# Attention on one core: the values' product of two quads of heads in one run, and eight buffers of probabilities in place of four

## The reference, cut to what matters

```python
def _L1_attn_ref(hidden_states, Wq, bq, Wk, bk, Wv, bv, Wo, bo):
    HEADS, HEAD_DIM = 16, 8
    ...                                   # q, k, v = linear(hidden_states), split into heads
    scores = jnp.einsum('bqhd,bkhd->bhqk', q * SCALE, k)
    probs = jax.nn.softmax(scores.astype(jnp.float32), axis=-1).astype(scores.dtype)
    out = jnp.einsum('bhqk,bkhd->bqhd', probs, v).reshape(b, s, d)
    return out @ Wo.T + bo
```

## Time and profile before

| | |
|---|---|
| median of 3 runs | 1103.3 us (1101.86 to 1104.05) |
| span of the profiled execution, first to last instruction | 1072.1 us |
| outside of the span, by the median | 31.2 us |
| PE busy | 963.4 us, 90% of the span |
| DVE, ACT, POOL busy | 706.6, 640.7, 707.7 us |
| `values` (L1518), matmul records | 2048, 141.6 us busy |

### The profile page before, as it was taken

How to read it: one execution, slowest core, us unless ns; L and a number is a source line. 1 busy time by engine, 2 the same in 40 slices (tenths; PEclk the granted TensorE clock), 3 DMA queues, 4 the chain that set the end, 5 groups by cost and what they waited for, 6 DMA issues and landing times. The chain is left out here.

```text
span 1072.1 us, 29674 instructions
## 1 busy us (share of the span) xinstructions
PE 963.4 (90%) x9857; PEld 717.1 (67%) x9858; DVE 706.6 (66%) x1509; ACT 640.7 (60%) x1320; POOL 707.7 (66%) x1531
## 2 busy tenths in 40 slices
PE   6999999689989999459999999999999999963776
PEld 5888888479956666335767777777777777632554
DVE  5778787685534444236788887788787788735752
ACT  4666766422224434126788888888888888762552
POOL 4677676467735555567688888888888888534003
PEclk9999999799999999757999999999999999996999
DMA  8600000131123332134444544445454445302000
GB/s 315 262 3 2 2 2 2 45 104 53 50 74 83 81 83 70 52 106 132 122 137 140 149 130 141 127 137 150 124 149 124 124 134 140 99 17 61 12 3 21
DMA packets 88837, 100.91 MB, mean 94 GB/s; under 512 B 10654, under 2 KB 74366, under 8 KB 88318
## 3 DMA queue, kind: packets, MB, share of 16 engines
q1 hardware_dynamic: 83454, 87.97, 27.9%
q0 software_dynamic: 5248, 11.15, 3.2%
HBM read 61.78 MB, written 36.47 MB: 92 GB/s over the span
## 5 line engine op out<-in xcount | busy, mean ns | idle before, releaser
L1344 DVE TENSOR_REDUCE a_neg_max<-a_slot 128x4 f32<-128x1024 f32 x256 | 306.5, 1218 | 107.8 <-PE a_slot L1487 83.3
L1432 ACT ACTIVATE a_pT<-a_slot 128x1024 f32<-128x1024 f32 x256 | 255.3, 1024 | 13.5 <-PE a_slot L1503 6.5
L1487 PE MATMUL a_slot<-a_k_stack,a_q_stack 72*128 72x256 bf16 x1024 | 157.9, 278 | 7.3 <-DMA a_k_stack<-part_dram 6.3
L1503 PE MATMUL a_slot<-a_q_stack,a_k_stack 75*128 75x256 bf16 x1024 | 151.0, 275 | 2.0 <-ACT a_pT L1432 0.7
L1518 PE MATMUL a_ps_o<-a_pT,a_v_pad 128*32 128x256 f32 x2048 | 141.6, 386 | 0.0
L1487 PEld LDWEIGHTS a_slot<-a_k_stack,a_q_stack 72*128 72x128 bf16 x1024 | 95.5, 99 | 51.9 <-issue 25.5
L704 POOL DMA_INDIRECT y_rows<-m_total,m_token x80 | 76.6, 957 | 66.3 <-ACT m_total L857 52.4
L1503 PEld LDWEIGHTS a_slot<-a_q_stack,a_k_stack 75*128 75x128 bf16 x1024 | 93.0, 98 | 35.5 <-ACT a_pT L1432 14.2
L326 DVE TENSOR_TENSOR r_score<-ps_score,r_decay 128x512 f32<-128x512 f32 x128 | 81.4, 678 | 7.7 <-PE ps_score L478 7.6
L1518 PEld LDWEIGHTS a_ps_o<-a_pT,a_v_pad 128*32 128x32 f32 x2048 | 64.7, 109 | 27.5 <-issue 13.0
L697 POOL DMA_INDIRECT sorted_in<-h,m_slot x64 | 63.9, 998 | 26.1 <-issue 18.9
(11 more groups left out here) (293 smaller groups left out, 2121.7 us busy)
## 6 DMA issues: line engine op xcount, KB each, us to landing
a_q_stack<-part_dram SPq DMA_DIRECT2D x64, 288.0 KB
a_k_stack<-part_dram SPq DMA_DIRECT2D x64, 288.0 KB
part_dram<-a_part SPq DMA_DIRECT2D x64, 192.0 KB, 2.7
sorted_in<-h SPq DMA_DIRECT2D x10, 528.0 KB, 13.6
m_xe<-sorted_in SPq DMA_DIRECT2D x40, 132.0 KB, 2.2
expert_up<-in_eu_dram SPq DMA_DIRECT2D x1, 4096.0 KB, 25.1
part_dram<-a_part SPq DMA_DIRECT2D x64, 64.0 KB, 3.6
out_dram<-e_x_plus_h SPq DMA_DIRECT2D x32, 128.0 KB, 2.5
```

Source lines behind the costliest of these rows:

```text
L1344: nc.vector.tensor_reduce(neg_max[:, p, half, t, g * UNIT:(g + 1) * UNIT], slots[SLOT_OF["m", j]][:], AX.X, ALU.max, negate=True).then_inc ...
L1432: nc.scalar.activation(pT[:, j % PT_RING], slots[SLOT_OF["e", j]][:], ACT.Exp).then_inc(e_read, 1)
L1487: ins = nc.tensor.matmul(slots[SLOT_OF["m", j]][:, q], q_stack[0:QK_ROWS, p, half, head, t * P:(t + 1) * P], k_stack[0:QK_ROWS, p, half, h ...
L1503: ins = nc.tensor.matmul(slots[SLOT_OF["e", j]][:, q], k_stack[0:EXP_ROWS, p, half, head, t * P:(t + 1) * P], q_stack[0:EXP_ROWS, p, half, ...
```

## The change

Three edits. `pT` gets one buffer for each of the eight units of a sequence in place of four. The wait of an exponential on the values' product that last read its buffer is moved by one sequence to match. In PE's list, VALUES(2) moves from behind e7 to stand with VALUES(3) behind `transpose_max(1)`, and VALUES(0) moves from behind `by_token` to stand with VALUES(1) behind `transpose_max(0)`; the lags are kept.

```diff
-PT_RING = 4
+PT_RING = M_UNITS
...
-                    after(act, o_done, AG * s + j // 2 - 1)
+                    after(act, o_done, AG * (s - 1) + j // 2 + 1)
...
             pipeline(pe, [(for_exponential(6), 5), (project_v, 2), (for_maximum(7), 4), (for_exponential(7), 5),
-                          (values(2), 5), (for_maximum(0), 3), (transpose_o, 6), (for_exponential(0), 4),
+                          (for_maximum(0), 3), (transpose_o, 6), (for_exponential(0), 4),
                           (for_maximum(1), 3), (output, 6), (for_exponential(1), 4), (for_maximum(2), 3),
-                          (transpose_max(1), 4), (values(3), 5), (transpose_h, 1), (for_exponential(2), 4),
-                          (for_maximum(3), 3), (for_exponential(3), 4), (by_token, 5), (values(0), 4),
+                          (transpose_max(1), 4), (values(2), 5), (values(3), 5), (transpose_h, 1), (for_exponential(2), 4),
+                          (for_maximum(3), 3), (for_exponential(3), 4), (by_token, 5),
                           (for_maximum(4), 3), (project_qk, 1), (for_maximum(5), 3), (for_exponential(4), 4),
-                          (for_maximum(6), 3), (transpose_max(0), 3), (values(1), 4),
+                          (for_maximum(6), 3), (transpose_max(0), 3), (values(0), 4), (values(1), 4),
                           (for_exponential(5), 4)], B, B)
```

## The result

The changed kernel takes 1155.38 us (median of 4 runs, 1154.62 to 1155.82) against 1102.58 us (1101.83 to 1104.05) on the same chip: ratio 1.0472, 95% interval 1.0454 to 1.0490, so some 52 us slower. The forecast was 1146 us in a range of 1136 to 1158.

A forecast was written before the change was run, and what follows sets the result against it. PE, busy 14.67 of 14.67 us a turn, seemed the bound, but the moved calls covered ACT's and DVE's chains. Added quads +56.3, forward moves -3.2, -4.2, -3.9, ends -2: +43 on 1103.3, forecast 1146 us, range 1136 to 1158.

The forecast's parts named there:

- seams: Around a call of values on PE: 0.22 us each, two a turn removed, 64 in all, 14 us.
- VALUES(2): Between e7 and m0: without it PE stalls about 1.0 us for ACT; e5 to e0 becomes 3.88 us, e0 0.1 forward.
- VALUES(0): Between by_token and m4: without it PE stalls about 0.9 us for DVE; m3 to project_qk becomes 2.86 us.
- added quads: Behind transpose_max(1) and transpose_max(0): each values call there gets 0.88 us longer, +56.3 us over the phase.
- small gain: At e1 behind output: m0 is filled and reduced sooner, so e1 comes forward 0.13 us a turn, -3.9 us.
- `project_qk` forward: Behind m3 and m4: project_qk could move forward 0 to 0.30 us; the middle, 0.15, was taken, -4.2 us.
- The ends: First turn without normalise holding project_qk, last three without project_qk: part of 1.10 us comes back, -2 us in all.
- the seams alone: Rival: PE-bound, both chains have room, so the kernel gets 14 us faster, 1089 us (1095 if POOL limits); 4 in 100.
- one chain alone: Rival: only ACT's chain holds, 1119 us, or only DVE's chain holds, 1114 us; 4 in 100.
- no net effect: Rival: the stalls come to just 0.22 us at each place; 1 in 100.
- further engine: Rival: POOL, whose pad_v waits for VALUES(3), adds 9 us, 1155 us; 3 in 100 together with the clock case.
- fall of the clock in the new holes: Rival: half clock through 3 of the 32 turns gives 1188 us; 3 in 100 together with the POOL case.

The follow-up runs named there:

- e7: In these lines PE's unit filling the slot for exponential 7; the run of that label, changed kernel with both reorderings (e5 and e6), has ratio 1.0423 to the kernel before.
- e4: Changed kernel with transpose_h put between VALUES(2) and VALUES(3), cutting that run of 32 into two of 16; ratio 1.0540 to the kernel before.
- e5: In these lines PE's unit filling for exponential 5; the run: changed kernel, two units before project_qk, VALUES(0)/VALUES(1) before transpose_max(0); ratio 1.0322 to kernel before.
- e9: Changed kernel with exponential 6 taken of two heads instead of four and used twice, PE's work unchanged; ratio 1.0411 to the kernel before.
- e10: Kernel before with exponential 6 taken of two heads instead of four and used twice; ratio 1.0005.
- e11: Changed kernel with the maximum of unit 3 taken over 128 keys instead of 256; ratio 1.0404 to the kernel before.
- e1: As a run, e1_buffers: kernel before with only the eight buffers and moved wait, ratio 1.0011; at the small gain, PE's unit behind output.
- e12: Kernel before with the maximum of unit 3 taken over 128 keys instead of 256; ratio 0.9935.
- e3_v0_only: Kernel before with the eight buffers and moved wait, and only VALUES(0) moved, to VALUES(1); ratio 1.0284.
- e2: Kernel before with the eight buffers and moved wait, and only VALUES(2) moved, to VALUES(3); ratio 1.0232.
- e8: Changed kernel with VALUES(2) back in place, VALUES(0) and VALUES(1) ahead of transpose_max(0), two units ahead of project_qk; ratio 1.0265 to the kernel before.
- e6: Changed kernel with m1 moved ahead of e0, and the run of VALUES(2) and VALUES(3) moved ahead of m2; ratio 1.0692 to the kernel before.

## Why the prediction was right, and where it was off

The mechanism held at each step but one, the room that `project_qk` was given (below). The **seams** are worth 0.23 us a run (predicted 0.22, shown by e4). **VALUES(2)** leaves a stretch of 3.88 us, predicted 3.88; m0 comes 2.68 us behind e5, predicted 2.7; shortening ACT's chain alone moves the changed kernel and not the one before (e9, e10). **VALUES(0)** leaves DVE's chain bare, with 1.1 us of waiting a turn in the list and 1.25 from start to start (predicted about 0.9; e11 shows whose chain it is). The **added quads** cost 0.90 and 0.85 (0.88 to 0.92 counted to e2), predicted 0.88 each. The **small gain** at e1 is 0.13, as predicted. The **buffers** are free (e1). One sign was misread ahead: PE's wait for ACT was to show under L1432 with 25 to 30 us, and shows as two lines of 8.5 us put down to "issue", since the list sees only idle time that the matmuls' ends do not cover.

The time was 9 us too low, mainly from two terms:

- *`project_qk` forward, 0.15 us a turn.* It came forward by nothing (3.01 us both times). I took half of the 0.36 us between DVE's end and the start as room and put the slow step from m4 down to PE's own semaphore waits. It was a stall already: e12 takes 0.16 us out of this step and 0.06 out of the next. `project_qk` starts 0.36 us behind the end of the product whenever PE stands there, not the 0.06 of the earlier trace rows. With this at zero, 14.67 + 0.90 + 0.85 - 0.10 - 0.13 = 16.19; measured 16.24. The turn as measured is 0.19 us over the 16.05 predicted, for 27 turns 5 us.
- *The ends, -2 us.* Against `e1_buffers`, whose trace is comparable, the last starts of `project_qk` lie 495.5 - 450.8 = 44.7 us further from the first, of which 27 steady turns make 42.2 and the first four 2.5; and from there to the last `output` it is 7.4 us more (59.5 against 52.1). So the ends cost 9.9 us where 5.7 were foreseen (the +43 of the sum less 27 turns of 1.38). At both ends the clock has a part in it. The turn at the start that answers to the first window above, and the last turns, of `e1_buffers`:

```profile
516.00:532.00 16.00, 15.48 (x153) 10.70 (x153) 11.78 (x15) 11.02 (x18) 10.28 (x24) 0.97 0.37 100
927.00:980.00 53.00, 47.46 (x496) 30.12 (x494) 32.57 (x55) 37.94 (x59) 25.26 (x62) 1.00 0.23 67
```

and the last turns of the changed kernel (its first is the first window above, with 0.80):

```profile
974.00:1035.00 61.00, 50.22 (x510) 33.29 (x510) 32.89 (x57) 38.39 (x60) 25.75 (x64) 0.94 0.21 61
```

In that first turn of the changed kernel the run of values, without its first three records, is at the lower of the two levels, 1.2 GHz, where 1.93 us for all 32 is usual:

```profile
521.04 3.48 PE L1518 MATMUL a_ps_o<-a_pT,a_v_pad 128*32 128x256 f32 x29
524.45 1.05 PE L1503 MATMUL a_slot<-a_q_stack,a_k_stack 75*128 75x256 bf16 x8
```

The products are at full clock again from 524.45, 8.0 us after the turn's `project_qk` (516.45). This turn takes 19.7 us against 15.1 in `e1_buffers`, but the one ahead of it 14.9 against 17.3, so of the 4.6 us only some 2.5 are left over the first four. In the last turns 6.8 us (1012.35 to 1019.18) have a granted clock of 0.50, and `e1_buffers` has none below 1.00 up to its last `output`; at half clock that is up to 3.4 us, by my estimate, of the 7.4. With VALUES(0) moved alone the turn at the start is long too (19.3 us in e3_v0_only), with VALUES(2) alone it is not (16.1). Why the clock rises later there, and dips in the last turns, was not tried.

Of the rivals, the seams alone, one chain alone and no net effect are excluded by the result and by e2 and e3. The further engine did not come in the changed kernel: POOL's wait for VALUES(3) shows with 0.3 us a turn (7.4 us in 25 turns), as costed, and no wait of PE answers to it; it did come in e8. The fall of the clock in the new holes did not come in the steady turns, where the granted clock is 1.00 in the window above, and came in small at both ends; in e6 it came in full, four times. That it spared the steady turns was not given by the argument of the prediction, a window with PE busy for 15.35 of 20 us at full clock: e6 lost it behind a turn with 14.61 of 16.90. The 31.2 us around the span were wrong as an account of the trace, but the sum is a difference and does not rest on them.

## What to carry to other kernels

In a list of steps that is filled to the last place, a step also stands as the cover of somebody else's chain: before it is moved, follow the next wait behind its old place to the engine that ends it, and ask what PE does in that time without it. A saving per seam (0.22 us here) is worth less than the cover (1.0 us and more). A PE that is busy for 14.67 of 14.67 us can still be waiting, so its steps from start to start must be compared with the usual ones. And when a step is put into the hole instead, follow the queues of all engines that read from it: of my four covers one failed on DVE's order (e6) and one on POOL and SP (e8), which had no room.

## What the runs showed of the hardware that I had not expected

- A product that PE was held for by a semaphore starts 0.36 us after the releasing instruction's end in the profile (702.06 to 702.42; 763.25 to 763.61), where e0 starts 0.10 us after its own (755.47 to 755.57). In its code `project_qk` waits on further semaphores behind that of `normalise`; that these are the difference was not tried.
- Half an exponential (512 of 1024 elements a partition) took 0.34 us off the changed kernel's turn. Half a reduction took off 0.33 us, though the reduction itself fell by 0.53 us (1.22 to 0.69): in e11 the reciprocal starts at 757.52, 0.12 us behind the end of the reduction and just behind that of `by_token` (757.48), which takes over as the next link.
- In e6 the granted clock fell from 1.00 to 0.50 four times, each time within 0.4 us of the end of a stand of PE of 1.1 to 1.2 us for `normalise`; ahead of the first, PE was busy for 14.61 of 16.90 us. In the steady turns of the changed kernel, with 14.46 of 16.20 us and a stand of 1.09 us at the same place, it stayed at 1.00. What makes the difference was not tried.
